# Node rows and walk tables of a graph network: two stages made one, table work placed in the node loop

## The reference, cut to what matters

```python
xn = _layernorm(x, axis=-1)
h = (xn @ W1).reshape(n, 4, 128)
al_s = jnp.einsum('nhc,hc->nh', h, a_src)
al_d = jnp.einsum('nhc,hc->nh', h, a_dst)
logits = leaky_relu(al_s[src] + al_d[dst], 0.2)      # per edge, softmax over the edges of one target
out = segment_sum(h[src] * alpha[:, :, None], dst)   # the walk over the edges
```

## Time and profile before

| | us |
|---|---|
| median of 3 runs | 6163.82 |
| lowest and highest run | 6153.75, 6172.43 |
| the profiled execution | 6173.5 |
| its span, first to last instruction | 6171.7 |

### The profile page before, as it was taken

How to read it: one execution, slowest core, us unless ns; L and a number is a source line. 1 busy time by engine, 2 the same in 40 slices (tenths; PEclk the granted TensorE clock), 3 DMA queues, 4 the chain that set the end, 5 groups by cost and what they waited for, 6 DMA issues and landing times. The chain is left out here.

```text
span 6171.7 us, 87850 instructions
## 1 busy us (share of the span) xinstructions
PE 4328.9 (70%) x20635; PEld 3204.3 (52%) x20636; DVE 3208.3 (52%) x8723; ACT 2796.2 (45%) x8562; POOL 3500.6 (57%) x3692
## 2 busy tenths in 40 slices
PE   7388888888888886746666666655555134999990
PEld 4266666666666665534444444444444123666660
DVE  3477767777777776744455554544444421222222
ACT  3367667676766675344444444433333011222220
POOL 0477777777777774067777777777776043000006
PEclk9699989999999998878777778777777557999995
DMA  4688888888888886445555555556664314111105
GB/s 159 182 242 243 242 237 241 238 244 240 242 243 242 242 243 197 141 133 140 141 142 141 141 141 140 136 158 165 166 169 123 127 53 165 35 34 33 33 29 167
DMA packets 700203, 1007.30 MB, mean 163 GB/s; under 512 B 385852, under 2 KB 489369, under 8 KB 699503
## 3 DMA queue, kind: packets, MB, share of 16 engines
q0 software_dynamic: 234384, 745.96, 41.6%
q1 hardware_dynamic: 458450, 249.00, 14.7%
q10 hardware_dynamic: 6924, 7.45, 0.4%
HBM read 904.69 MB, written 90.97 MB: 161 GB/s over the span
## 5 line engine op out<-in xcount | busy, mean ns | idle before, releaser
L806 POOL DMA_INDIRECT walk_ring<-s_h,walk_index x3320 | 3208.3, 966 | 1296.7 <-issue 929.2
L967 PE MATMUL walk_pM<-walk_ring,walk_hit 128*128 128x262 f32 (+1 forms) x9960 | 2769.0, 431 | 11.6 <-ACT walk_ring L831 6.9
L967 PEld LDWEIGHTS walk_pM<-walk_ring,walk_hit 128*128 128x128 f32 x9960 | 2029.4, 212 | 419.1 <-issue 75.1
L831 ACT ACTIVATE walk_ring<-walk_ring 128x128 f32<-128x128 f32 (+1 forms) x6640 | 2134.4, 414 | 5.4
L1197 DVE TENSOR_TENSOR acc<-walk_pM,acc 128x520 f32 (+1 forms) x1494 | 833.8, 558 | 583.3 <-PE walk_pM L967 562.0
L821 ACT ACTIVATE walk_ring<-walk_gap 128x40 f32<-128x40 f32 (+1 forms) x249 | 54.1, 258 | 1915.2 <-DVE walk_gap L1159 1915.2
L871 PE MATMUL walk_pC<-all_ident,walk_best 128*84 128x128 f32 (+1 forms) x166 | 62.3, 375 | 1079.2 <-DVE walk_best L1115 924.1
L871 PEld LDWEIGHTS walk_pC<-all_ident,walk_best 128*84 128x84 f32 (+1 forms) x166 | 20.7, 125 | 1141.7 <-issue 1141.7
L1164 DVE TENSOR_TENSOR walk_hit<-walk_pK,walk_meta 128x512 f32<-128x512 f32 x830 | 561.1, 676 | 12.4 <-PE walk_pM L967 1.0
L1115 DVE TENSOR_TENSOR walk_best<-walk_ring,walk_dt 128x40 f32<-128x40 f32 (+1 forms) x249 | 47.0, 217 | 876.9 <-DMA walk_ring<-s_h,walk_index 876.9
L1851 ACT ACTIVATE expert_hT<-expert_pG,expert_b 128x128 f32<-128x128 f32 x840 | 229.3, 383 | 576.7 <-PE expert_pG L1914 576.5
(11 more groups left out here) (300 smaller groups left out, 3906.4 us busy)
## 6 DMA issues: line engine op xcount, KB each, us to landing
walk_hitT<-s_places SPq DMA_DIRECT2D x166, 640.0 KB
walk_ring<-s_h,walk_index POOLq DMA_INDIRECT x3320
expert_w<-in_fw_dram POOLq DMA_DIRECT2D x16, 1024.0 KB, 7.8
s_xs<-finish_zero POOLq DMA_DIRECT2D x30, 448.0 KB, 18.6
expert_xin<-s_xs SPq DMA_DIRECT2D x105, 128.0 KB, 2.0
s_ys<-expert_out POOLq DMA_DIRECT2D x105, 128.0 KB, 2.0
walk_goal<-walk_target SPq DMA_DIRECT2D x830, 6.0 KB
walk_goal<-walk_target SPq DMA_DIRECT2D x830, 1.5 KB
```

The source lines that it names most:

```text
L806: pool.indirect_dma_start(ring[:, r % RS, t, :], None, table, bass.IndirectOffsetOnAxis(ap=index[:, r % TS, t:t + 1], axis=0)).then_inc(ro ...
L831: last = nc.scalar.activation(row, row, ACT.Copy, scale=ring[:, r % RS, t, at + FH:at + FH + 1])
L967: last = nc.tensor.matmul(pM[:, b, a, 0:WIDE], hit[:, (r * CGROUPS + g) % HBUF, t % GROUP, :], ring[:, r % RS, t, a * HALF_ROW:a * HALF_RO ...
```

## The change

`first_pass` takes the place of `node_pass` and `edge_pass`: one block with the buffers and semaphores of both. The work of the node loop is as before. What differs:

- SP issues the DMA of the first targets ahead of the loads of `x`, and the stores of the tables at the beginning of trips 2 (windows), 4 (places, resets, through) and 6 (meta, index) of its loop over seven tiles, each behind a wait for its table.
- Row statistics go by parts of ten tiles. Part 0 comes before the loop, part 1 in tile 0, the others two tiles at a time in the second half of each ten. Variances of part c+1 are made in tile 10c, the root by ACT at the end of its tile 10c, the inverse roots in tile 10c + 2.
- DVE does the search for rows ahead of the attention weights and the other table steps at fixed tiles: ends in tile 1, the plan in 4, windows in 8, the eight steps over the edges in tiles 12 to 19, one table copied in each of tiles 22 to 42.
- PE spreads the ends in tile 3, turns the windows in tile 7, and turns one table (two transposes) in each of tiles 22 to 42, ahead of the tile's product. The tables go through two PSUM banks in turn, where before six were used.
- POOL's two fetches wait as before, for DVE's row and plan.

`newton`, called with ten columns, is the same chain of reciprocal and five small operations as L265 to L274.

```diff
-def node_pass(nc, k, d):
-
+def first_pass(nc, k, d):
...
+        pT = m.ps("pT", [P, 2, 512])
+        pH = m.ps("pH", [P, 2, F1])
+        pA = m.ps("pA", [P, 2, 512])
         pF = m.ps("pF", [P, 512])
-        pO = m.ps("pO", [P, 512])
-        pT = m.ps("pT", [P, 2, 3, 512])
+        pE = m.ps("pE", [P, 512])
+        E = TPS * P
+        firsts, ends, turned_w = pF[:, 0:P], pF[:, P:P + NW], pF[0:SJ, 2 * P:3 * P]
+        tables = [a[:, 0:TPS * P] for a in (pF, pE)]
+        XP = 10
+        XPARTS = [(c, min(c + XP, NT)) for c in range(0, NT, XP)]
+        TABLES = [(j, n) for j in range(SJ) for n in range(3)]
+        T_ENDS, T_WALK, T_WINDOWS, T_PLACE, T_TURN = 1, 4, 8, 12, 22
...
+                for (lo, hi), sem in zip(XPARTS, loaded):
+                    sp.dma_start(x[:, lo:hi, :], d["x"].rearrange("(t p) c -> p t c", p=P)[:, lo:hi, :]).then_inc(sem, 16)
+
+                def store_tables(i):
+                    if i == 2:
+                        sp.wait_ge(windows_ready, 1)
+                        sp.dma_start(d["windows"].rearrange("(j p) -> j p", p=P), windows[:, :]).then_inc(tables_out, 16)
+                    if i == 4:
+                        sp.wait_ge(places_ready, 1)
+                        sp.dma_start(d["places"].rearrange("(j p) e -> p j e", p=P), place_b[:, :, :]).then_inc(tables_out, 16)
+                        sp.wait_ge(resets_ready, 1)
+                        for u in range(TPS):
+                            for way in range(2):
+                                sp.dma_start(d["resets"].rearrange("(j p) u w e -> p j u w e", p=P)[:, :, u, way, :],
+                                             reset[:, :, u * P + way:(u + 1) * P + way]).then_inc(tables_out, 16)
+                        for way in range(2):
+                            sp.dma_start(d["through"][way, :].rearrange("(j p u) -> p j u", p=P, u=TPS), through[:, way, :, :],
+                                         allow_slow_non_contiguous=True).then_inc(tables_out, 16)
+                    if i == 6:
+                        sp.wait_ge(table_copied, len(TABLES))
+                        sp.dma_start(d["meta"].rearrange("p a t -> p (a t)"), meta[:, :, :, :].rearrange("p a s u -> p (a s u)")).then_inc(tables_out, 16)
+                        sp.dma_start(d["index"], index[:, :, :].rearrange("p s u -> p (s u)")).then_inc(tables_out, 16)
+
+                for i in range(TRIPS):
+                    store_tables(i)
+                    for s, (lo, hi) in enumerate(UPARTS):
+                        tiles = slice(i * U + lo, i * U + hi)
+                        sp.wait_ge(row_ready, i * U + hi)
+                        sp.dma_start(d["h1"].rearrange("(t p) c -> p t c", p=P)[:, tiles, :], h_out[:, lo:hi, :]).then_inc(stored[s], 16)
+                        sp.dma_start(d["xT"].rearrange("t p c -> p t c")[:, tiles, :],
+                                     xT[:, lo:hi, :, :].rearrange("p t k n -> p t (k n)")).then_inc(stored[s], 16)
...
+                def root(c):
+                    lo, hi = XPARTS[c]
+                    act.wait_ge(stats_done, c + 1)
+                    nc.scalar.activation(half[:, lo:hi], var[:, lo:hi], ACT.Sqrt, bias=eps[:, 0:1]).then_inc(root_done, 1)
...
+                    nc.scalar.copy(heads[:, :, :, P], k["attn1"][:, t, 0:HEADS1].rearrange("p (a h) -> p a h", a=2)).then_inc(row_ready, 1)
+                    if t % XP == 0 and t // XP + 1 < len(XPARTS):
+                        root(t // XP + 1)
...
+                def measure(c, tiles):
+                    dve.wait_ge(loaded[c], 16)
+                    for t in tiles:
+                        nc.vector.bn_stats(stats[:, t, :], x[:, t, :])

+                def variances(c):
+                    lo, hi = XPARTS[c]
+                    dve.drain()
+                    nc.vector.tensor_tensor(mean[:, lo:hi], stats[:, lo:hi, 1], stats[:, lo:hi, 4], ALU.add)
...
+                def inverse_roots(c):
+                    lo, hi = XPARTS[c]
+                    dve.wait_ge(root_done, c + 1)
+                    newton(nc, dve, rstd[:, lo:hi], half[:, lo:hi], var[:, lo:hi])
...
+                def prepare_norm(t):
+                    if t == 0:
+                        measure(1, range(*XPARTS[1]))
+                    c = t // XP + 2
+                    if c < len(XPARTS) and t % XP >= XP // 2:
+                        lo, hi = XPARTS[c]
+                        first = lo + 2 * (t % XP - XP // 2)
+                        measure(c, range(first, min(first + 2, hi)))
+                    c = t // XP + 1
+                    if c < len(XPARTS) and t % XP == 0:
+                        variances(c)
+                    if c < len(XPARTS) and t % XP == 2:
+                        inverse_roots(c)
...
+                def find_ends():
+                    dve.wait_ge(run_in, 16)
+                    nc.vector.tensor_copy(run[:, :], run_i[:, :])
+                    dve.drain()
...
+                def plan_walk():
+                    dve.wait_ge(ends_out, 1)
+                    nc.vector.tensor_copy(bound_i[:, :], ends)
...
+                def edge_step(n):
+                    if n == 0:
+                        dve.wait_ge(edges_in, 16 * SJ)
+                        nc.vector.tensor_tensor(place[:, :, :], edges[:, :, 1:E + 1], spread(lift[:, :], 2, E), ALU.subtract)
+                    if n == 1:
+                        nc.vector.tensor_tensor(same[:, :, :], edges[:, :, 0:E + 1], edges[:, :, 1:E + 2], ALU.is_equal)
+                    if n == 2:
+                        nc.vector.tensor_copy(src[:, :, :], edges[:, :, E + 2:])
+                        dve.drain()
+                    if n == 3:
+                        nc.vector.tensor_copy(place_b[:, :, :], place[:, :, :]).then_inc(places_ready, 1)
+                    if n == 4:
+                        nc.vector.tensor_scalar(last_one[:, :, :], same[:, :, 1:], -1.0, 1.0, ALU.mult, ALU.add)
+                    if n == 5:
+                        nc.vector.tensor_scalar(reset[:, :, :], same[:, :, :], -1.0, BIG, ALU.add, ALU.mult)
+                        dve.drain()
+                        dve.sem_inc(tables_ready, 1)
+                    if n in (6, 7):
+                        for way in range(2):
+                            nc.vector.tensor_reduce(through[:, way, :, n - 6], reset[:, :, (n - 6) * P + way:(n - 5) * P + way], AX_X, ALU.min)
+                        dve.drain()
+                    if n == 7:
+                        dve.sem_inc(resets_ready, 1)
+
+                def copy_table(q):
+                    j, n = TABLES[q]
+                    dve.wait_ge(table_turned, q + 1)
...
+                def edge_work(t):
+                    if t == T_ENDS:
+                        find_ends()
+                    if t == T_WALK:
+                        plan_walk()
+                    if t == T_WINDOWS:
+                        keep_windows()
+                    if T_PLACE <= t < T_PLACE + 8:
+                        edge_step(t - T_PLACE)
+                    if T_TURN <= t < T_TURN + len(TABLES):
+                        copy_table(t - T_TURN)
+
+                nc.vector.memset(eps[:, :], EPS)
+                nc.vector.memset(h_out[:, :, :].rearrange("p u (a c) -> p u a c", a=2)[:, :, :, 2 * (P + 1):], 0.0).then_inc(tails_cleared, 1)
+                list_firsts()
+                measure(0, range(*XPARTS[0]))
+                variances(0)
+                find_rows()
+                attention_weights()
+                inverse_roots(0)
+                for t in range(U):
+                    norm(t)
+                for t in range(NT):
+                    dve.wait_ge(multiplied, t + 1)
+                    nc.vector.tensor_copy(k["attn1"][:, t, :], pA[:, t % 2, 0:2 * HEADS1]).then_inc(a_copied, 1)
+                    if t + U < NT:
+                        norm(t + U)
+                    prepare_norm(t)
+                    edge_work(t)
...
+                def edge_work(t):
+                    if t == T_ENDS + 2:
+                        pe.wait_ge(ends_ready, 1)
+                        nc.tensor.matmul(ends, k["ones"][:, :], diag[:, :], start=True, stop=True).then_inc(ends_out, 1)
+                    if t == T_WALK + 3:
+                        pe.wait_ge(walk_ready, 1)
+                        nc.tensor.transpose(turned_w, at_window[:, :], k["ident"][:, :]).then_inc(windows_turned, 1)
+                    if T_TURN <= t < T_TURN + len(TABLES):
+                        q = t - T_TURN
+                        j, n = TABLES[q]
+                        if q == 0:
+                            pe.wait_ge(tables_ready, 1)
+                            pe.wait_ge(windows_ready, 1)
+                        if q >= 2:
+                            pe.wait_ge(table_copied, q - 1)
+                        for u in range(TPS):
+                            last = nc.tensor.transpose(tables[q % 2][:, u * P:(u + 1) * P], (place, last_one, src)[n][:, j, u * P:(u + 1) * P],
```

(28 more changed lines are left out.)

346 lines of the change are left out of this document (122 added, 224 removed).

## The result

The changed kernel takes 6105.96 us in the median (6101.26 to 6114.31); the kernel before takes 6162.93 us (6153.75 to 6172.43) beside it. The ratio is 0.9913 with an interval of 0.9901 to 0.9925: faster by 57.0 us, where 59.8 were forecast. The profiled execution of after took 6109.92 us, with a span of 6108.3 us against 6171.7.

The account below looks back on a forecast made before the run. The edge walks' gathers are the largest group but unchanged; PE bounds the node loop. Removed 66.6 + 13.4, added 4.9 + 13.4 + 1.9: 59.8 us off the median 6163.8, so 6104.0 us, range 6085 to 6123.

Parts of the forecast that it names:

- The table stage: The stage between node loop and walk goes, from its first issue to the walk's first issue: 66.6 us off.
- The start: Ahead of the node loop: only ten tiles are measured first, so TensorE starts at 27.6 us, 13.4 us earlier.
- What TensorE gets more: Node loop: 21 tables of two transposes at 0.21 us each, 0.5 for ends and windows; 4.9 us added.
- First tile: Tile 0: ten statistics and variances delay ACT's root and the transposed copies queued behind it; PE waits 3.4 us.
- The ends: Tile 1: DVE's ends cost 3.5 us and PE's product of tile 3 queues behind them; wait of 1.2 us.
- Tiles 12 to 20: DVE's edge steps, statistics and roots exceed its room, then tile 20's variances; about 4.2 us with the small waits before.
- Tile 34 (35 in the text): Tile 35: node stores queue behind places, resets and through in one ring; wait 3.2 to 6.8 us, 3.7 taken.
- The hidden part: Loop's end: stores of meta and index drain behind it, POOL's work costs nothing; 2 to 4 us if cover fails.
- The chain of guests (A): Rival, chance 0.18: late edges push DVE's work beyond tile 20, SP waits at places; 10 to 20 us more, 6119.
- The swallowed waits (B): Rival, chance 0.14: the loop's waits are mostly swallowed and only 4.9 us are added; gain 75, 6089 us.
- The clock over the whole loop (C): Rival, chance 0.02: waits and transposes spread over the loop keep TensorE at 1.2 GHz; +33 us, 6197.
- D: Rival, chance 0.02: the walk's start is bound by something that doesn't move with the stage; no change, 6164.

Follow-up runs that it names:

- the POOL kernel: The changed kernel with places, resets and through issued by POOL on its own queue instead of by SP: 6102.42 us in one run.
- the spacing: The changed kernel with DVE's eight edge steps at tiles 11, 13 to 17, 21 and 23 instead of 12 to 19: 6105.32 us in one run.
- The first experiment: The changed kernel with the two stores of through moved from trip 4 to trip 6, behind meta and index: 6110.5 us in one run.
- the repeated kernel: The changed kernel run once more, unchanged: median 6109.6 us, ratio 0.9918 to the kernel before.

## Why the prediction was right, and where it was not

**The table stage, right.** 66.6 us off, and nothing took its place as a whole. The tail, from the last row copy to the next stage, is 8.3 us against 7.6.

**The start, 0.7 too high in all.** TensorE's first tile stands at 29.33, 11.7 us earlier than at 41.00, not 13.4. The first part of x is measured from 15.91 and not 14.3: the stage's first issue moved from 4.26 to 5.28 with 18 more semaphores to clear, 1.0 us where 0.3 was taken, a term for which the text had no row. The list of the first rows kept the queue for another 0.75 us, and x landed 9.9 us after its own first issue (6.03) instead of 9.0 (from 4.26 to 13.29), for which no run shows the cause (timeline of DVE in after):

```profile
15.91 3.37 DVE L343 BATCH_NORM_STATS2 first_stats<-first_x 128x6 f32<-128x256 f32 x10 [5.81 <-DMA first_x<-in_x_dram]
19.36 0.18 DVE L348 TENSOR_TENSOR first_mean<-first_stats 128x10 f32<-128x10 f32 x1
...
20.29 0.34 DVE L400 TENSOR_SCALAR_CACHE_REDUCE first_below<-first_pF,first_top 128x128 f32<-128x128 f32 x1
```

The variances took 0.93 us, the low bound of 0.9 to 1.7 (1.2 taken). What the sum did not have is that the first product ran in 3.06 us instead of 3.78, as the clock rose during it, so the first row copy is 12.7 us earlier. That is luck: in the other runs of this code it took between 3.01 and 3.78 us. What the merge costs at the start shows beside the kernel with only the statistics per part: its first row copy stands at 30.56, 3.4 us ahead of the 33.98 in after, and the text had 1.8 us for it (1.0 for the queue and the clears, 0.8 for the search).

**What TensorE gets more, right**: 2.55 instead of 2.34 per table, 0.21 each, 4.4 in all, as read from the earlier trace rows. The product of the ends is the 0.2 us of tile 3; the turn of the windows stands in a wait and shows nowhere, so 4.6 of the 4.9 came.

**The waits: the sum right, the terms less so.**
- First tile: 3.4 forecast, PE waited 2.91. Right, with its mechanism; the tile's product at half clock, 3.68, came on top. The text counted one such product for the whole loop, arguing that here the clock was low anyway. That step failed: the clock had risen by 34.06, where a product took 1.88.
- The ends: 1.2 forecast, no wait measured, because the first wait and the slow product behind it had covered them. Where that product ran at full clock, in the POOL kernel, PE waited 0.59 us for the ends; the kernel with the merge alone shows the uncovered price, 1.35 us of waiting and 1.7 of clock.
- The plan: 0.9 and 0.9.
- Edges in time: right; no wait of DVE for them at tile 12.
- Tiles 12 to 20: 4.2 forecast; 13, 14 and 20 to 22 cost 2.8 more than before. The cause given was DVE's budget. That is the smaller part: at tile 13 ACT waits for a store and not for DVE (2.12 us, 1.35 before), and at tile 20 DVE's terms are 1.30 us late, but the store awaited behind them also landed later, 6.7 us after its issue at 82.30 instead of 5.9 before, and the spacing left 3.74 us there. Only the wait for the variances behind tile 20 came as described. A sum near the measured one, by a cause that is less than half of it.
- Tile 34 (35 in the text): 3.7 forecast, 6.2 measured, and 1.6 of clock behind it, where 1.9 was forecast. The mis-sized term is through. The text took 2.2 of the 5.8 us of the earlier trace rows for it, because the next table was read as flowing in that stretch; it held the DMA engines for 6.5 us in after, at 83 GB/s in the mean. The high bound was the price, and the wait 6.8 forecast from it is close to the 6.2. The trace of before already spoke for it. Meta was issued there at 219.40, but for most of the time until 224 hardly anything moved (windows view of before, columns as in the earlier trace rows):

```profile
221.75:222.50 0.75, 0.00 (x0) 0.00 (x0) 0.00 (x0) 0.00 (x0) 0.00 (x0) 0.50 0.00 0
...
223.25:224.00 0.75, 0.00 (x0) 0.00 (x0) 0.00 (x0) 0.00 (x0) 0.00 (x0) 0.50 0.32 76
224.00:224.75 0.75, 0.00 (x0) 0.00 (x0) 0.00 (x0) 0.00 (x0) 0.00 (x0) 0.50 0.89 268
```

  The other terms held. Resets had moved by some 120.5, 12.3 us behind the store at 108.20, where 13.0 was forecast, although SP took 7.71 us to issue them instead of 3.59; the data of the four tiles, 4.1 us by a figure for which the text names no row, were through some 3.5 us after 127. The reason given, the order of one ring, fell with the POOL kernel.

Together: the forecast had 13.4 of waits, 1.9 of clock and 4.9 for PE, 20.2 us in the loop; 21.1 were measured. With the first row copy 0.7 less early than forecast and a tail 0.7 longer, the three misses make 59.8 - 0.9 - 0.7 - 0.7 = 57.5. Behind that small difference single terms were off by 1 to 4 us, and they cancelled: that the forecast of 6104.0 lies 2 us from the median is luck to that extent.

**The hidden part, right.** meta and index are issued at 154.33, and no engine waits for them. The first experiment shows how thin the cover is: 14 KB more behind them cost 4.7 us.

**The rivals.** The chain of guests (A) didn't come: edges in time, SP never held at places. The swallowed waits (B) didn't either. The clock over the whole loop (C) didn't: 0.96 from 34 to 168; but it is the part of every wait that the forecast underrated. The walk's start moved with the stage, so D is out.

One thing stays open. Why the stores of tiles 14 to 17, which ACT awaits at tile 20, are slow wasn't found: before, too, ACT's longest wait in the loop was for them (1.65 us, at 93.62 us). In after the edge gathers are issued from 53.38 to 61.84, well ahead of these stores, so they are not the cause.

## What to carry to other kernels

Before work is put beside a loop that one engine bounds, count the room of every buffer ring around it as well as the time of the other engines: a store that is already awaited for 1 us in the shadow leaves none for a second stream. Price a store of many tiny pieces by how long it holds the DMA engines, not by its bytes, and issue it in small portions that stand apart; another queue didn't help here. A short wait of TensorE can cost as much again in clock, though it doesn't always: one of 1.4 us was worth 3.

## What the runs showed of the hardware

- Two stores of 14 KB in all, in pieces of 8 bytes, with the stores of the loop close behind them, kept the 16 DMA engines busy at a low rate for some 6.5 us from SP's queue and 7.0 from POOL's. Issued one by one, in the kernel with the stores spread, the first left a low rate of 2 us behind it (41 and 114 GB/s from 127 to 129). This is the window over both in after:

```profile
120.50:127.00 6.50, 5.32 (x26) 3.17 (x24) 3.15 (x14) 1.40 (x5) 0.00 (x0) 1.00 1.07 83
```

- TensorE's granted clock fell behind waits much shorter than those of the earlier trace rows: after 1.35 us (product 3.58 us instead of 1.88, in the merge alone), 1.61 us (3.35, the POOL kernel), 1.93 us (2.72, the repeated kernel) and 2.13 us (2.98, the stores spread). It did not fall behind others as long: in after a wait of 1.63 us at tile 20 was followed by a product of 1.98, and in the POOL kernel one of 2.65 us at tile 1 as well. So the length of a single wait doesn't tell; what does was not tried.
- Under load SP took 7.71 us to issue the four stores of resets, and 3.59 in the table stage before, where no store of the loop stood ahead of them.
- A semaphore more in the stage's start costs some 57 ns: 18 more, 1.02 us (4.26 to 5.28), and one more again, in the POOL kernel, 0.05 (5.33).
